# Gate product of the RWKV numerator moved from VectorE to GpSimd, into the next chunk's step

## The reference, cut to what matters

```python
# layer 1: RWKV time mixing (x shifted by one token is xx)
k, v, r = (x*mix + xx*(1-mix)) @ W.T          # three mixes, three matrices
sr = sigmoid(r)                                # the gate
wkv: for every token t and channel
    no = max(o, u + kt);  A = exp(o - no);  Bc = exp(u + kt - no)
    y  = (A * p + Bc * vt) / (A * q + Bc)      # numerator / denominator
    no2 = max(w + o, kt); p, q, o = the carried sums, rescaled
x = layernorm(x + (sr * y) @ Wo.T)
# layer 2: mixture of experts, 8 experts, best 2 per token
logits = x @ Wg + bg;  top 2, softmax over the two scores
y_e = act(x @ W1[e] + b1[e]) @ W2[e] + b2[e]   # gelu on even, silu on odd experts
x = layernorm(x + sum of the two experts' outputs, weighted)
```

## Time and profile before

| | |
|---|---|
| median of 3 runs | 773.06 us (771.36 to 774.31) |
| the profiled execution | 775.2 us |
| its span | 773.4 us |
| busy, share of the span | PE 84%, DVE 59%, ACT 51%, POOL 38% |
| L1174, the product with the gate | 8 times, 9.9 us in all |

### The profile page before, as it was taken

The page is one execution under the profiler, slowest core; times in us unless marked ns, Lnnn a source line. Parts: engine busy times, 40 slices in busy tenths (PEclk is TensorE's granted clock), DMA queues, the critical chain, the costliest instruction groups (busy, mean ns, idle before and its releaser), DMA issues.

```text
span 773.4 us, 14741 instructions
## 1 busy us (share of the span) xinstructions
PE 648.2 (84%) x4512; PEld 605.9 (78%) x4512; DVE 453.3 (59%) x960; ACT 395.2 (51%) x717; POOL 295.3 (38%) x299
## 2 busy tenths in 40 slices
PE   4979799999976516999999999999999999999000
PEld 3858688788855416999999999999999999999000
DVE  3748889999996353844545345455464354442584
ACT  2545576576662103645546446456646546453374
POOL 4000116446555542525327263263461361212364
PEclk9998899999976657999999999999999999999555
DMA  8200221322122266661413214214141111201793
GB/s 262 80 28 1 81 82 56 111 81 99 67 75 97 91 176 206 198 228 39 152 51 115 86 43 151 58 33 153 50 159 49 39 46 43 57 12 34 232 309 123
DMA packets 56610, 78.39 MB, mean 101 GB/s; under 512 B 5174, under 2 KB 46083, under 8 KB 56356
## 3 DMA queue, kind: packets, MB, share of 16 engines
q1 hardware_dynamic: 40468, 50.54, 19.9%
q0 software_dynamic: 6496, 16.99, 6.3%
q10 hardware_dynamic: 9520, 9.25, 4.5%
HBM read 49.14 MB, written 28.40 MB: 100 GB/s over the span
## 4 chain that ended last, share of the span: by engine, by line
PE 73%; DVE 10%; issue 7%; ACT 3%; DMA 3%; POOL 2%; another core or an unknown queue 0%; SPq 0%; ACTq 0%; DVEq 0%; POOLq 0%
PE hT_ps L800 25%; PE y_ps L809 25%; PE vr_ps L670 8%; PE k_ps L670 7%; PE wo_ps L678 3%; PE xT_ps L823 2%; DVE o_all L1081 1%; DVE dest L1309 1%; PE small_ps L692 1%; POOL rstd_c L637 1%; PE xT_ps L661 1%; DVE xl L1159 1%; DMA yy<-expert_out_dram 1%; DMA records_dram<-rec,slot_i 1%; ACT res L1032 1%
## 5 line engine op out<-in xcount | busy, mean ns | idle before, releaser
L800 PE MATMUL hT_ps<-xTh,wx 128*128 128x256 f32 x1120 | 210.7, 286 | 0.4 <-issue 0.3
L809 PE MATMUL y_ps<-wx,aTh 128*128 128x256 f32 x1088 | 197.4, 283 | 0.9 <-DVE y_sb L1299 0.9
L800 PEld LDWEIGHTS hT_ps<-xTh,wx 128*128 128x128 f32 x1120 | 177.5, 192 | 1.3 <-issue 0.7
L1323 DVE TENSOR_TENSOR aTl<-hT_ps,aTh 128x512 fp32r<-128x512 f32 x140 | 93.3, 688 | 135.4 <-ACT aTh L991 135.4
L809 PEld LDWEIGHTS y_ps<-wx,aTh 128*128 128x128 f32 x1088 | 169.7, 192 | 1.1 <-issue 1.1
L618 POOL DMA_INDIRECT expert_out_dram<-y_sb,dest x70 | 68.3, 976 | 253.8 <-DVE y_sb L1299 239.0
L800 PE MATMUL hT_ps<-xTl,wx 128*128 128x256 f32 x560 | 158.7, 283 | 0.0
L809 PE MATMUL y_ps<-wx,aTl 128*128 128x256 f32 x544 | 154.0, 283 | 0.0
L985 ACT ACT_TABLE_LOAD x35 | 44.9, 1283 | 191.8 <-PE hT_ps L800 177.6
L985 ACT ACTIVATE hT_ps<-hT_ps,b_c 128x256 f32<-128x256 f32 x280 | 113.4, 469 | 0.8 <-PE hT_ps L800 0.3
L800 PEld LDWEIGHTS hT_ps<-xTl,wx 128*128 128x128 f32 x560 | 107.8, 192 | 0.0
(11 more groups left out here) (181 smaller groups left out, 870.0 us busy)
## 6 DMA issues: line engine op xcount, KB each, us to landing
staging<-in_L_ffn_W SPq DMA_DIRECT2D x16, 1024.0 KB
recs<-records_dram ACTq DMA_DIRECT2D x35, 258.0 KB
yy<-expert_out_dram SPq DMA_DIRECT2D x16, 512.0 KB, 5.3
xin<-in_L_attn_x SPq DMA_DIRECT2D x16, 256.0 KB, 4.4
xres<-in_L_attn_x SPq DMA_DIRECT2D x16, 256.0 KB, 3.0
x_dram<-rec SPq DMA_DIRECT2D x16, 256.0 KB, 3.3
xx<-x_dram SPq DMA_DIRECT2D x2, 2048.0 KB, 18.4
out<-res SPq DMA_DIRECT2D x16, 256.0 KB, 3.6
```

Of the source, the lines that this page charges most:

```text
L800: ins = pe.matmul(hT_ps[b][:, f, :], wx[:, s, part, off:off + P], xpart[t.slot % 2][:, cc, :], start=k == 0, stop=k == len(terms) - 1)
L809: ins = pe.matmul(y_ps[h], apart[t.slot % 2][:, fc, h * P:(h + 1) * P], wx[:, s, part, off:off + C], start=k == 0, stop=k == len(terms) - 1)
L1323: dve.tensor_tensor(aTl[u.slot % 2][:, 2 * b:2 * b + 2, :], hT_ps[b][:], aTh[u.slot % 2][:, 2 * b:2 * b + 2, :].bitcast(F32), ALU.subtract ...
```

## The change

The product with the gate leaves VectorE's `numerator(i)` and becomes `apply_gate(c)` on GpSimd, called first in GpSimd's step c + 1. It waits for the numerator (`num_done`), for the gate (`gate_out`) and, where there is a step c + 1 with a chunk of its own, for `o_carry` of that chunk, that is until VectorE is about to begin the scans of the next chunk. `divide(c)` waits for `gated_done` ahead of L1109 as before; the semaphore now comes from GpSimd. Behind the changed place the changed kernel's line numbers are 8 to 10 higher (L1109 is L1119, L583 is L591).

```diff
--- before.py
+++ after.py
@@ -558,6 +558,14 @@
                 pool.tensor_tensor(wx[:, 0, 1, at], raw[:, at], wx[:, 0, 0, at].bitcast(F32),
                                    ALU.subtract).then_inc(weights_ready if last else piece_lo, 1)
 
+            def apply_gate(c):
+
+                pool.wait_ge(num_done, c.upto(1))
+                pool.wait_ge(gate_out, c.upto(CC))
+                if (c + 1).exists:
+                    pool.wait_ge(o_carry, (c + 1).upto(1))
+                pool.tensor_tensor(num[:], num[:], gate[c.slot][:], ALU.mult).then_inc(gated_done, 1)
+
             def spread_of(c):
                 pool.wait_ge(mv_done, c.upto(J))
                 pool.tensor_tensor(var_e[:], mv[:, :, 1], eps_b[:], ALU.add).then_inc(vare_done, 1)
@@ -586,6 +594,8 @@
                             oob_is_err=False).then_inc(rec_out[at], 16)
 
             def step(i):
+                if (i - 1).exists:
+                    apply_gate(i - 1)
                 if i.exists:
                     split_piece(i)
                 early = i - 3
@@ -1169,9 +1179,6 @@
                 dve.wait_ge(ev_done, i.upto(1))
                 dve.wait_ge(p_done, i.upto(1))
                 dve.tensor_tensor(num[:], bonus[:], p_all[:, :, :, 0:TC], ALU.add).then_inc(num_done, 1)
-                dve.wait_ge(num_done, i.upto(1))
-                dve.wait_ge(gate_out, i.upto(CC))
-                dve.tensor_tensor(num[:], num[:], gate[i.slot][:], ALU.mult).then_inc(gated_done, 1)
 
             def statistics(c):
                 dve.wait_ge(res_done, c.upto(2))
```

## The result

| | before | after |
|---|---|---|
| median | 773.88 us (771.36 to 776.78, 6 runs) | 783.22 us (782.54 to 785.02, 6 runs) |
| ratio to before | | 1.0113, 95% interval 1.0093 to 1.0133 |
| profiled span | 773.4 us | 781.6 us |

The change makes the kernel slower by 1.1%, some 9 us; 783.4 was predicted. A second measurement of the same kernel beside the experiments gave 1.0132 (1.0114 to 1.0150).

The account below looks back on a forecast made before the run. TensorE was taken to pace the middle and the drain to wait on others; the span's 773.4 plus 10.35 for the held product of chunk 7 gave 783.75, the same shift on the 773.06 median 783.4, range 780.5 to 787.0.

Parts of the forecast that it names:

- TensorE paces the middle: Steps 0 to 6: removing VectorE's 1.24 us product gives 0, since its next instruction then waits longer.
- Step 7 gives 0.7 us: Step 7, `residual_1` behind L1174: about 1.2 us could be had, falling to 0.7 us.
- the meeting: GpSimd's moved weight-piece subtraction blocks VectorE's newton L1102 in each step: 0.5 us later, bounds 0 and 1.3.
- The product takes 2.40 us: GpSimd's added 128x1024 product: 2.40 us from a line through 512 and 4096 columns, bounds 2.28 and 2.56.
- It is hidden in chunks 0 to 6: GpSimd's product of chunks 0 to 6 runs under the next step's scans, 4 us to spare: cost 0.
- In the drain it is held by the eight issues: Chunk 7's product waits behind `send_records(5)` on GpSimd, so L1109 starts 10.35 us later; bounds 9.9 to 11.0.
- The clock term: Drain: if TensorE's clock rose later, chunk 7's second projection would take 3.5 instead of 1.9 us; taken as 0.
- "Every gap as before": From the drain's idle time of about 10 us to the first phase's end, all gaps stay unchanged.
- The second phase as before: The second phase, which starts when all records have landed, stays as long as before.
- not held: Drain: product there by 236 us, only step 7's 0.7 us remains; 772.4, not slower; chance 0.03.
- VectorE paces the middle: Middle: each of six steps gives 0.77 us, so the shift is 5.7 and the time 778.8; chance 0.06.
- the meetings cost more: Steps 1 to 7: scans pushed behind the product, 8.1 us more, 791.5; chance of 788 or more 0.09.

Follow-up runs that it names:

- the second pair of profiles: The changed kernel and the kernel before, each measured once more without an edit: 785.68 us for the changed kernel, span 773.7 for the kernel before.
- `divide(7)` first: VectorE's divide(7) ahead of place(5): ratio 0.9974 with all products on GpSimd and chunk 7's ahead of the issues, 0.9955 in the kernel before.
- four ahead: Changed kernel with GpSimd's product of chunk 7 behind four of the eight record issues of chunk 5: 785.47 us, ratio 1.0128.
- two ahead: Changed kernel with GpSimd's product of chunk 7 behind two of the eight record issues of chunk 5: 777.69 us, ratio 1.0018.
- pieces early: Changed kernel with chunk 7's product ahead of chunk 5's issues, plus the seven later weight pieces split in step 0: 777.30 us, ratio 1.0023.

## Why the prediction was right

**TensorE paces the middle, so seven removals give nothing.** Shown. The waits of `residual_1` grew, the version without any product was no faster there than versions at the same clock, and seven of eight products moved made a ratio of 1.0003.

**Step 7 gives 0.7 us (1.2 less 0.5 for the meeting).** The mechanism is shown, both sizes were too high: the removal gave 0.90, the meeting cost 0.30, and the changed kernel had 0.52 us. The overlap came as forecast: the weight piece ended at 216.26, 0.45 us behind the newton instruction's start. But the instruction was longer by only 0.30 us (1.52 us in step 7, 1.44 to 1.52 in the seven steps, where about 1.7 was forecast); a whole restart behind that end would have made it 1.67.

**The product takes 2.40 us.** 2341 to 2407 ns, median 2392. The line through the rows for 512 and 4096 columns held, although it was drawn from subtractions.

**It is hidden in chunks 0 to 6.** Shown by the version with chunk 7 back on VectorE.

**In the drain it is held by the eight issues, 10.35 us in all.** The mechanism is shown, by taking it away, by doing it alone, and by the count. The term was mis-sized: from the end of `place(5)` the hold grew by 12.34 us, while the sum had 255.6 - 242.14 - 2.41 = 11.05. The 1.29 us between them are the first issue: it starts 1.29 us behind `place(5)` and takes 2.04, where it was 0.97 and 1.08 before (together 1.28 us more).

**The clock term, 0 to +1.6, taken as 0.** The right sign and within its bound: 0.48 us, from L1109 or L1119 to the end of the second projection. TensorE got 2.4 GHz from the scores on in both kernels; in the changed one it fell back during the second projection (granted clock 0.50 in 262 to 263 us), whose eight matmuls took 2.78 us instead of 1.97; they had started 0.33 us sooner behind the newton instruction.

**"Every gap as before" behind L1109.** Wrong in one gap. The prediction named a shrinking stretch between the idle time and the second phase as a sign of being wrong, and it shrank, from 49.72 to 48.76 us. It held that nothing in this row is independent of L1109. The chain of waits in the kernel before has a link that is: "250.57 3.16 another core or an unknown queue", ahead of `choose(6)`. That start was 1.69 us behind the scores and the changed kernel's 0.17; the 1.52 us between them are more than the 0.48 that the clock cost. What holds `choose(6)` is not shown. Only the two profiles of the kernel before have it; the view of the DMA traffic lists one instruction packet (queue q8) in each, at 251.2 and at 250.7, between the residual and the late start. Four other versions have one there too, but their scores end later, so they don't decide it, and no run tried it.

**The second phase as before.** 478.43 and 478.62 us.

So the 783.4 came out of errors that partly cancel. In the profiles the shift was 8.20 us and not 10.35: the hold was 1.29 too small, the clock 0.48 too small, and the late `choose(6)` (some 1.6) and the way to step 7 (2.85, of which the second pair of profiles leaves 1.45) went the other way with no term for them. The median shifted by 9.34 us, from a median before of 773.88 where the prediction started at 773.06. That the sum of these met the median to 0.2 us is luck; the range of 780.5 to 787.0 is what the argument could carry.

Of the rivals, *not held* fell with the trace, and is what the version with the product ahead of the issues does; *VectorE paces the middle* fell with the version without a product and the table by clock; *the meetings cost more* fell with the 0.3 us and with chunk 7 back on VectorE.

## What to carry to other kernels

Before work moves to an engine that is idle on the average, read that engine's order at the place where the result is wanted: an idle engine with in-order issues is not a free one, and one late instruction in the pipeline's drain can cost more than seven hidden ones save. A step that repeats is judged in the steady part and at the end apart, since the stages that stand around it differ. Where a small edit moves the time, the marks in the trace, not the time, tell which part of it is the edit's.

## What the runs showed that was not expected

**TensorE's clock is worth some 3 us in the drain.** From the third newton instruction of chunk 7 TensorE's work is the same everywhere: eight matmuls, the scores, eight matmuls. (With `divide(7)` first it begins 0.7 us later, behind transposes.) Up to its end it took 8.73 to 9.41 us in eight profiles (the kernel before's two, 8.77 and 8.75, among them) and 12.27 or 12.28 in the five others (product ahead, four ahead, two ahead, pieces early, no product). The timeline of TensorE in the changed kernel and in the version with the product ahead of the issues:

```profile
255.06 3.57 PE L688 MATMUL wo_ps<-wo,newton 128*128 128x256 f32 x8 [14.49 <-DVE newton L1119]
258.55 0.40 PE L699 MATMUL small_ps<-bg_b,ones 1*128 1x32 f32 x2
258.88 1.95 PE L702 MATMUL small_ps<-wg,x1T 128*128 128x8 f32 x16
```

```profile
243.51 3.75 PE L690 MATMUL wo_ps<-wo,newton 128*128 128x256 f32 x8 [2.25 <-DVE newton L1121]
247.20 0.63 PE L701 MATMUL small_ps<-bg_b,ones 1*128 1x32 f32 x2
247.76 3.58 PE L704 MATMUL small_ps<-wg,x1T 128*128 128x8 f32 x16
251.19 3.76 PE L690 MATMUL wo_ps<-wo,newton 128*128 128x256 f32 x8
```

Before all of it the granted clock is 0.50, 1.2 GHz. The changed kernel, idle for 14.49 us, gets 2.4 GHz from the scores on, until it falls back in the second projection; the other, idle for 2.25 us, has 1.2 GHz to the end of the second projection. The version with four issues ahead was idle for 10 us and had 1.2 GHz too, and the one with chunk 7 back on VectorE was idle for 2.80 and had 2.4 GHz from the scores on. So the length of the idle time ahead doesn't decide it; what does is open. It goes with the scatter of the times, too: of the twelve runs of the version with chunk 7 back on VectorE the slowest, 779.86 us, had the lowest mean granted clock, 0.897, and the fastest, 773.01, had 0.908. A single profile of a version need not be its usual run.

**The first record issue of chunk 5 has two lengths.** It took 2.04 or 2.05 us, and started 1.29 or 1.30 us behind `place(5)`, in the change and in the versions with two and four issues ahead and with chunk 7 back on VectorE; 1.06 to 1.09 us and 0.97 to 0.99 behind in all others, the kernel before among them. Both profiles of the change have it. In the order of GpSimd's program the versions with the long issue have seven products ahead of it, those with the short one eight or none: the same code stands at other places in the program. That would fit a fetch of instructions at that place, and the view of the DMA traffic bears it out: it lists one packet of an instruction queue (q14) between 0.3 us ahead of that issue's start and 0.5 us behind it in all five profiles with the long issue, and none within 3 us of it in the other eight. Whose queue q14 is no view says, and no run moved the code to try it.
